# Merging the row statistics of eight rows in five vector operations

## The reference

```
def _layernorm(x, axis=-1, eps=1e-05):
    m = jnp.mean(x, axis=axis, keepdims=True)
    v = jnp.var(x, axis=axis, keepdims=True)
    return (x - m) / jnp.sqrt(v + eps)

x = _layernorm(x + _L0(...))   # hypergraph layer
x = _layernorm(x + _L1(...))   # two attention convolutions over 25,000 edges and self-loops
x = _layernorm(x + _L2(...))   # one plain graph convolution with batch normalization
x = _layernorm(x + _L3(...))   # two attention convolutions, a row normalization between them
```

## Time and profile before

| | |
|---|---|
| median of 3 runs | 6914.04 us (6909.73 to 6926.38) |
| the profiled execution | 6893.67 us, span 6891.9 us |
| DVE busy | 4801.2 us (70%), 15928 instructions |
| POOL busy | 3942.9 us (57%) |
| PE busy | 4268.4 us (62%) |
| ACT busy | 3299.1 us (48%) |
| `bn_aggr` of the edge layers (L2483) | 1176 |

### The profile page before, as it was taken

How to read it: one execution, slowest core, us unless ns; L and a number is a source line. 1 busy time by engine, 2 the same in 40 slices (tenths; PEclk the granted TensorE clock), 3 DMA queues, 4 the chain that set the end, 5 groups by cost and what they waited for, 6 DMA issues and landing times. The chain is left out here.

```text
span 6891.9 us, 79501 instructions
## 1 busy us (share of the span) xinstructions
PE 4268.4 (62%) x18989; PEld 3142.2 (46%) x18989; DVE 4801.2 (70%) x15928; ACT 3299.1 (48%) x7376; POOL 3942.9 (57%) x3167
## 2 busy tenths in 40 slices
PE   3568883048885878499766677988885677600000
PEld 1257772037774666387622223547774566500000
DVE  6634544645545777599599986866665999578766
ACT  0023331013332555288556665758884788633333
POOL 4767776757774887676154515611113565277776
PEclk9689996579997999799877778989998899855555
DMA  8744445955454999699588878989996677476675
GB/s 304 284 105 78 76 75 159 351 169 79 76 79 108 346 349 343 203 335 339 193 294 307 313 254 304 379 296 330 332 335 221 229 257 244 174 268 235 235 241 183
DMA packets 646114, 1634.09 MB, mean 237 GB/s; under 512 B 128454, under 2 KB 283878, under 8 KB 630290
## 3 DMA queue, kind: packets, MB, share of 16 engines
q1 hardware_dynamic: 459954, 1234.83, 51.7%
q0 software_dynamic: 185696, 394.18, 21.2%
HBM read 816.50 MB, written 813.62 MB: 237 GB/s over the span
## 5 line engine op out<-in xcount | busy, mean ns | idle before, releaser
L2303 ACT ACTIVATE l_z<-l_a,l_nb,l_rs 128x256 f32<-128x256 f32 x1176 | 609.1, 597 | 432.5 <-DMA out_dram<-l_z,k_ids 234.5
L822 POOL DMA_INDIRECT NS<-e_tot,e_idx x392 | 648.3, 1654 | 291.0 <-ACT e_tot L1080 213.3
L1691 POOL DMA_INDIRECT l_eg<-HBT,k_nsrc x392 | 467.7, 1193 | 404.6 <-DVEq L1916 166.1
L956 DVE TENSOR_SCALAR e_eq<-e_pk,z_skey 128x128 f32<-128x128 f32 x588 | 203.9, 347 | 630.2 <-DMA NS<-e_tot,e_idx 599.9
L2180 POOL DMA_INDIRECT out_dram<-l_z,k_ids x392 | 419.9, 1071 | 143.0 <-issue 118.0
L1734 PE MATMUL l_pb<-l_jx,k_ones 128*128 128x128 f32 x26 | 4.3, 304 | 789.4 <-issue 785.2
L2225 PE MATMUL l_pm<-k_w_L3b,l_zt 128*128 128x258 f32 x1568 | 405.2, 417 | 127.6 <-ACT l_o L2273 127.6
L1080 ACT ACTIVATE e_tot<-e_pa 128x520 f32<-128x520 f32 x196 | 118.5, 605 | 752.2 <-DMA NS<-e_tot,e_idx 739.9
L1223 POOL DMA_INDIRECT XH<-n_o,z_home x392 | 397.1, 1013 | 121.6 <-issue 113.6
L2474 DVE BATCH_NORM_STATS2 l_bs<-l_a 128x6 f32<-128x256 f32 x1176 | 452.6, 408 | 13.2 <-DMA l_a<-X 5.3
L2199 PE MATMUL l_ps<-l_a,k_ident 128*128 128x512 f32 x392 | 298.1, 852 | 234.0 <-DVE l_a L2448 204.2
(11 more groups left out here) (405 smaller groups left out, 13510.1 us busy)
## 6 DMA issues: line engine op xcount, KB each, us to landing
NS<-z_zero SPq DMA_DIRECT2D x200, 520.0 KB
HBT<-l_o SPq DMA_DIRECT2D x196, 528.0 KB
l_a<-HBT SPq DMA_DIRECT2D x196, 528.0 KB
GSUMS<-l_erun SPq DMA_DIRECT2D x72, 1056.0 KB
l_a<-XH SPq DMA_DIRECT2D x98, 528.0 KB
HA<-n_o SPq DMA_DIRECT2D x98, 528.0 KB
l_a<-HA SPq DMA_DIRECT2D x98, 528.0 KB
n_r<-NS SPq DMA_DIRECT2D x98, 520.0 KB
```

The source lines that it names most:

```text
L822: pool.indirect_dma_start(out=nodes, out_offset=bass.IndirectOffsetOnAxis(ap=idx[q % DEEP][:, k:k + 1], axis=0), in_=tot[q % 2][:, k, :], ...
L1691: pool.indirect_dma_start(out=self.g[b % self.ng][:, k, :], out_offset=None, in_=self.table, in_offset=bass.IndirectOffsetOnAxis(ap=self.i ...
L2303: last = act.activation(z[:, j, 0:D], a[:, j, 0:D], ACT.Identity, bias=self.nb[b][:, col:col + 1], scale=self.rs[b][:, col:col + 1])
```

## The change

In `Nodes.variance` the eight `bn_aggr` are replaced by operations over all eight rows at once. With means m1, m2 and sums of squared differences q1, q2 of the two halves of a row (128 elements each), the mean is (m1 + m2)/2 and the variance is (q1 + q2 + (D/4)(m1 - m2)^2)/D. Three operations read `bs` (the tile of six floats per row, so with a step of 24 bytes): gap = m1 - m2, mv0 = m1 + m2, mv1 = q1 + q2. Two more make (D/4) gap^2 and add it to mv1. The division by D moves into the operation that adds epsilon, and the half of the mean into the constant of `shifts`. The tile `gap` is new. There is a yield behind each of the five, so `variance` now takes six turns of its tick and not five. A `settle` stands ahead of the last two of the five and of the epsilon operation.

```diff
+            self.gap = [s.sb(f"gap{b}", [P, 2 * J]) for b in range(2)]
...
-        for j in range(2 * J):
-            self.var_lk.link(dve.bn_aggr(self.mv[b][:, j, :], self.bs[b][:, j, :]))
-            if j % 2:
-                yield
-        self.var_lk.settle(dve)
+        lk, bs, mv, ve, gap = self.var_lk, self.bs[b], self.mv[b], self.ve[b], self.gap[b]
+        lk.link(dve.tensor_tensor(gap[:], bs[:, :, 1], bs[:, :, 4], ALU.subtract))
+        yield
+        lk.link(dve.tensor_tensor(mv[:, :, 0], bs[:, :, 1], bs[:, :, 4], ALU.add))
+        yield
+        lk.link(dve.tensor_tensor(mv[:, :, 1], bs[:, :, 2], bs[:, :, 5], ALU.add))
+        yield
+        lk.settle(dve)
+        lk.link(dve.scalar_tensor_tensor(gap[:], gap[:], float(D // 4), gap[:], ALU.mult, ALU.mult))
+        yield
+        lk.settle(dve)
+        lk.link(dve.tensor_tensor(mv[:, :, 1], mv[:, :, 1], gap[:], ALU.add))
+        yield
+        lk.settle(dve)
         if q >= 2:
             dve.wait_ge(self.s_rs, q - 1)
-        dve.tensor_scalar(self.ve[b][:], self.mv[b][:, :, 1], EPS, None, ALU.add).then_inc(self.s_var, 1)
+        dve.tensor_scalar(ve[:], mv[:, :, 1], 1.0 / D, EPS, ALU.mult, ALU.add).then_inc(self.s_var, 1)
...
-        dve.scalar_tensor_tensor(self.nb[b][:], self.mv[b][:, :, 0], -1.0, self.rs[b][:], ALU.mult, ALU.mult).then_inc(self.s_nb, 1)
+        dve.scalar_tensor_tensor(self.nb[b][:], self.mv[b][:, :, 0], -0.5, self.rs[b][:], ALU.mult, ALU.mult).then_inc(self.s_nb, 1)
```

## The result

| | median | lowest to highest | runs |
|---|---|---|---|
| before | 6914.04 us | 6903.40 to 6926.38 | 7 |
| changed | 6887.39 us | 6866.10 to 6894.94 | 7 |

The ratio is 0.9963, with 0.9945 to 0.9982 as its 95% interval: 26 us less, and between 12 and 38. The forecast was 6890 us. So the time came out as predicted; whether for the reasons given is the question of what follows.

The account below looks back on a forecast made before the run. DVE was taken to bound l2 and l5, POOL's queue l6. A gain of 0.23 us per variance summed to 24 us, taking the median of 6914.04 us to 6890, with 8 in 10 runs from 6868 to 6916.

Parts of the forecast that it names:

- The bound: In l2 and l5 DVE sets the time, so each us saved shortens the span; in l6 POOL's queue sets it.
- The waits cost nothing: The three settles on DVE cost nothing behind a bn_stats of 0.31 us; uncovered they would cost 0.375 us per variance.
- The price of the removed work: Eight bn_aggr per variance on DVE, priced by distance to the next start: 0.155 us per double, 0.62 us for four.
- The price of the added work: Five operations of 8 floats on DVE at 0.075 us, plus 0.015 for the 24-byte step: 0.39 us per variance.
- the first rival: Small DVE operations with a 24-byte step cost 0.10 us each, leaving 10 us gain, 6904 us; chance 0.22.
- the first term: The 0.62 us per variance that removing eight bn_aggr was to take from DVE.
- The sum: Gains of 19.6 us in l2 and l5, 2.5 at their ends and 1.6 late in l6: together 24 us.
- Dear small operations: The added DVE operations cost 0.10 us each, so the gain is only 10 us, 6904 us; chance 0.22.
- Given back: A hand-over between ACT, PE and DVE sets the tick in l2, so time stays at 6912 us; chance 0.08.
- More in `l6`: Fewer instructions shorten l6's starved stretches, where DVE gets one each 0.7 us: 13 us more, 6877 us; chance 0.10.
- Moved stretches: DVE's starved stretches shift from l6 into l2 or l5: one gives 6915 us, two 6940 to 6950; chance 0.10.

Follow-up runs that it names:

- e3: Changed kernel without the yields between the five operations, so each settled one stands right behind the one it waits for: 6793.82 us, ratio 1.0055 to before.
- e4: Kernel before with a second bn_aggr into a spare tile behind each of the eight: 6801.41 us, ratio 1.0071 to before.
- e7: Kernel before with a tensor_tensor of 8 floats into a spare tile behind each bn_aggr: 6809.46 us, ratio 1.0080 to before.
- e2: Changed kernel with the five operations in l6 alone and the eight bn_aggr back in l2 and l5: 6753.91 us, ratio 0.9996 to before.
- e8: Kernel before with its eight bn_aggr together in one step, the four turns kept: 6757.81 us, ratio 1.0006 to before.
- e6: Changed kernel with statistics laid out column by column, so small operations read neighbouring floats and bn_stats writes with a step: 6895.51 us, ratio 0.9980 to before.
- r_changed: The changed kernel unaltered, timed a second time on a faster chip beside the kernel before: 6736.51 us, ratio 0.9975 to before.
- e1: Changed kernel with the eight bn_aggr back in l6 alone, the five operations kept in l2 and l5: 6740.74 us, ratio 0.9980 to before.
- e5: Changed kernel with m1 + m2 and q1 + q2 made by one operation of 16 floats, four operations for five: 6738.53 us, ratio 0.9976 to before.
- e10: Changed kernel with statistics laid out column by column and both additions in one operation of 16 floats: 6875.69 us, ratio 0.9953 to before.

## Why the prediction was right, and where it was not

**The bound, right.** `l2` and `l5` give back what DVE saves: in e3, e4 and e7 the two distances grew with DVE's work, and the time followed (e4: 44 us of work over the 84 `variance`, 47 us of time; e7: 56 and 55). In `l5`, where DVE is never idle, it is 1:1. In `l2` it is so only roughly: in e4 the work grew by 21.8 us and the distance by 15 to 17.5 (613.0 us, against 597.8 before and 595.5 in e2), as 4 to 6 us of idle time went. `l6` gives nothing that can be told from noise (e2, and e7 against e8).

**The waits cost nothing, right, and shown.** The changed kernel has no idle time ahead of the settled operations of `l2` and `l5`, and e3 shows what the `bn_stats` between them hides: 0.40 to 0.42 us per `variance`, where 0.375 was said. With that cover gone the change is a loss, as the prediction put it.

**The price of the removed work, wrong.** This is the term that failed: "What one takes from DVE is the distance to the next start [...] of many such doubles I take 0.155, so four are 0.62 us". The reading was true of the rows (their mean is 0.153 to 0.154), but removing the eight `bn_aggr` is worth only 0.52 us (e4). A part of such a distance is given back in the distance of the instruction behind: here 0.026 us for each of the four doubles (the 0.311 of the `bn_stats` behind them against 0.336), 0.10 in all, which is the error of 0.62 - 0.52. What is left of the gain is 0.10 to 0.13 us by these prices, and 0.11 by the profiles. Where every `bn_aggr` is doubled (e4), the first row's excess and the give-back are in both kernels and cancel.

**The price of the added work, right.** 0.39 us by the rows, 0.35 to 0.415 by e7 (without and with the lost give-back), where 0.39 was said, and the step of 24 bytes is worth the 0.015 put on it (e6). The Trainium skill ("SBUF — State Buffer", section Door 1), whose penalty for each new line of 16 bytes stood behind the first rival, is not contradicted, but the price is too small to matter here (0.005 us for eight floats). With the first term mended the gain is 0.11 us per `variance`, not 0.23, and over all 98 of `l2` and `l5` at most 11 us of DVE's work, not 22.

**The sum, right by luck in part.** DVE's work in the 42-`variance` stretches is about 9 us shorter in both phases together. The whole phases are 10.0 to 12.9 us shorter. Of the rest of the 12.9 some 2 us are idle time of DVE in `l2` (16.4 us before, 14.0 after, first chip), and the end of `l2` is 2.5 us shorter (59.8 to 57.3), that of `l5` 1.6 longer (58.6 to 60.2). The first timing's 26 us are 13 or more above that; its interval begins at 12, and the second and larger timing says 17. So the forecast of 24 us agrees with a 26 of which only half can be found in the phases: the sum was twice too large, and the first timing happened to lie as high. Where the other half comes from stays open. `l6` alone takes 799.7 to 813.7 us in the four profiles from chips as slow as the first, so one profile of each kernel cannot say. With 0.11 in place of 0.23 the sum would have been 11 us instead of 24 and the forecast 6903 us, 16 above what was measured and still inside the stated range.

**The rivals.** *Dear small operations*: its gain of 10 us was nearer to the mark than the forecast's 24, but for the wrong reason, as it is the removed operations that were cheaper. *Given back*: falls, since the phases shortened and DVE is as full as before. *More in `l6`*: its 13 us lie outside the interval of e2. But e2 and e7 ran on chips whose `l6` shows none of the starved stretches that this rival is about (see below). On the first chip it rests on one profile of each kernel, 812.0 us before and 813.7 changed. *Moved stretches*: they lie elsewhere now, still inside `l6`, where POOL covers them. One lies at 6466 to 6496 us (stretch, length, DVE busy):

```profile
6466.00:6496.00 30.00, 10.03 (x36) 0.50 0.72 254
```

and in it the settled operations start far apart, with idle time that the view puts down to a DMA (LIST) or to nothing. That DMA was issued at 391 us, long before, so it can't be what ended this wait:

```profile
6485.11 0.17 DVE L2494 TENSOR_TENSOR l_mv<-l_mv,l_gap 128x8 f32<-128x8 f32 x1 [1.23 <-DMA LIST<-e_listed]
6485.19 0.42 DVE L2475 BATCH_NORM_STATS2 l_bs<-l_a 128x6 f32<-128x256 f32 x1
6487.94 0.17 DVE L2516 SCALAR_TENSOR_TENSOR l_rt<-l_rt,l_ve 128x8 f32<-128x8 f32 x1 [2.33 <-issue]
```

None fell into `l2` or `l5` in any of the profiles, so the rival's price was never paid. Its premise, that the program's instructions decide where they lie, is at the least not the whole of it, since the same changed kernel has such stretches on one chip and none on another. The least busy 30 us of DVE between the first and the 43rd epsilon operation of `l6`, in the changed kernel on the first chip and then in r_changed:

```profile
6230.00:6260.00 30.00, 5.99 (x23) 0.50 0.50 170
```

```profile
6043.60:6073.60 30.00, 17.78 (x70) 0.50 0.72 246
```

All twelve profiles divide in this way. In the four from chips where the kernel before takes 6910 or 6914 us DVE is busy 4 to 6 us of its emptiest 30, in the eight from the chips of 6754 us 17 to 18. What makes the stretches was not tried.

## What to carry to other kernels

Price a removed instruction by a kernel that has it twice, or look at what the neighbour behind takes with it and without it, and do not rely on the distance to a neighbour of another kind: here that made 0.23 us of a gain of 0.11. A chain of small dependent operations was worth adding here because a `bn_stats` of 0.3 us of other work stood between its links; back to back the links cost 0.20 us each, and more than the change saves. How little work between them would do was not tried. And where the phase is bound by one engine, compare phases from mark to mark, since the work of that engine repeats to a few tenths of a us while whole runs spread over 30.

## What was not expected of the hardware

**The granted clock of `l2`.** In the rows of whole phases above PE does the same 774 matmuls in 465.38 us at a granted clock of 0.75 with the old merge and in 443.73 at 0.80 with the new one. Every profile agrees: 0.75 to 0.78 in `l2` for before, e2, e4, e7 and e8, 0.79 to 0.81 for the changed kernel (twice), e1, e5, e6 and e10, and 0.77 for e3, which has the new operations but the long ticks. Each of these is a mean over the two levels of 1.2 and 2.4 GHz; in `l6`, where PE is idle, it is 0.50. Most of `l2` is DVE's, so PE's 22 us can be worth no more than the few us of DVE's idle time and of the end of `l2` named above. Those 465 us are the most of all twelve profiles; on the first chip PE's time goes from 453 to 445 us. That a shorter tick of DVE raises the clock is a guess. It fits the two groups, but not the order within the first: e7 has the longest distance of all (621.8 us) at 0.78, e2 a short one (595.5 us) at 0.75. No run isolates it.

**The chip.** The kernel before takes 6914 us on one chip and 6754 on others. The changed kernel, profiled on both, has the same DVE work in `l2` and `l5` (576.7 and 576.9, 547.0 and 547.1 us). `l6` differs, 732.3 us against 689.5 between the same two marks, and with it DVE's idle time, 173 us against 134; the starved stretches stand in the profiles of the slower chips alone. `l2` begins 102 us earlier on the faster chip (3390.2 against 3491.8). So the phases that DVE binds repeat from chip to chip, and the one that POOL's queue of indirect DMAs sets does not. Why the chips differ was not tried.

**A neighbour that gives back.** That a `bn_stats` behind a `bn_aggr` takes 0.03 us less to the next start than behind a tensor_tensor, and the first `bn_aggr` of a group 0.03 us more than the ones behind it, is a reading of rows, if of many: 187 and 271 for the `bn_stats` of the kernel before and the changed one. Why it is so was not tried.
